# Routing of the second part of the expert stages: groups five blocks apart, loads one at a time, placing in two and sharing in five pieces

## What is computed

```python
h = _rms(x, ff_ln_w)
logits = h @ wg
...
gate = jax.nn.softmax(topv, -1)
...
weights = jnp.zeros_like(logits).at[bidx, sidx, topi].set(gate)
a = jax.nn.silu(jnp.einsum('bsd,edh->bseh', h, w1)) * jnp.einsum('bsd,edh->bseh', h, w3)
y = jnp.einsum('bseh,ehd->bsed', a, w2)
moe = jnp.einsum('bsed,bse->bsd', y, weights)
return x + moe
```

## Time and profile before

| What | Value |
|---|---|
| Median of three runs | 2684.96 us (2683.85 to 2685.91) |
| The profiled execution | 2682.36 us, its span 2680.6 us |
| Instructions | 60407 |
| TensorE busy | 2266.7 us, 85% |
| VectorE busy | 1855.2 us, 69% |
| ScalarE busy | 1159.6 us, 43% |
| GpSimd busy | 1103.8 us, 41% |
| Mean granted clock of TensorE | 0.90 |

### The profile page before, as it was taken

The page is one execution under the profiler, slowest core; times in us unless marked ns, Lnnn a source line. Parts: engine busy times, 40 slices in busy tenths (PEclk is TensorE's granted clock), DMA queues, the critical chain, the costliest instruction groups (busy, mean ns, idle before and its releaser), DMA issues. The chain is left out here.

```text
span 2680.6 us, 60407 instructions
## 1 busy us (share of the span) xinstructions
PE 2266.7 (85%) x20880; PEld 1718.4 (64%) x20880; DVE 1855.2 (69%) x3965; ACT 1159.6 (43%) x2509; POOL 1103.8 (41%) x1111
## 2 busy tenths in 40 slices
PE   6899999885887689995799998999988698999990
PEld 4555555543766567773577877777767577887770
DVE  4888888872556757765778788788787365445754
ACT  2676667664533223333344444444333263333330
POOL 3454445464153500000454454455477600224626
PEclk9897779865888889997999999999989799999995
DMA  5455555442368431201322323322334472446754
GB/s 118 120 115 129 143 129 135 114 125 87 113 215 252 150 134 41 60 29 40 88 66 75 84 66 78 81 72 73 76 96 116 136 240 79 138 137 184 234 159 144
DMA packets 249859, 313.10 MB, mean 117 GB/s; under 512 B 45152, under 2 KB 202848, under 8 KB 249056
## 3 DMA queue, kind: packets, MB, share of 16 engines
q1 hardware_dynamic: 188592, 219.11, 29.3%
q0 software_dynamic: 26624, 58.79, 8.0%
q10 hardware_dynamic: 34352, 31.34, 3.5%
HBM read 122.40 MB, written 102.24 MB: 84 GB/s over the span
## 5 line engine op out<-in xcount | busy, mean ns | idle before, releaser
L2084 POOL TENSOR_TENSOR ca_qk<-ca_qk,ca_q_swap 128x512 f32<-128x512 f32 x160 | 249.3, 1558 | 366.5 <-DVE ca_q_swap L2262 366.2
L731 DVE TENSOR_REDUCE soft_top<-soft_pa 128x2 fp32r<-128x512 f32 x512 | 328.1, 683 | 101.2 <-PE soft_pa L811 98.1
L626 ACT ACTIVATE soft_prob<-soft_pb 128x512 f32<-128x512 f32 x512 | 285.7, 594 | 190.4 <-PE soft_pb L804 187.9
L804 PE MATMUL soft_pb<-soft_rep 25*128 25x256 f32 x1024 | 210.2, 378 | 46.5 <-DVE soft_top L731 27.0
L804 PEld LDWEIGHTS soft_pb<-soft_rep 25*128 25x128 f32 x1024 | 137.3, 225 | 169.6 <-issue 85.3
L1416 PE MATMUL moe_pgu<-moe_w_hi,moe_xt_hi 128*128 x472 | 196.1, 415 | 38.9 <-DVE moe_xt_lo L1333 30.1
L811 PE MATMUL soft_pa<-soft_rep 24*128 24x256 f32 x1024 | 219.2, 384 | 5.8 <-DVE soft_top L731 3.5
L1435 PE MATMUL moe_py<-moe_w_d,moe_at 128*128 x788 | 217.8, 392 | 1.5 <-issue 0.8
L1338 DVE TENSOR_TENSOR moe_act_f<-moe_silu,moe_pgu 128x256 f32<-128x256 f32 (+1 forms) x236 | 88.4, 375 | 151.0 <-ACT moe_silu L1253 150.4
L2353 PE MATMUL ca_py<-ca_w_hi,ca_ot_hi 128*128 128x256 f32 x512 | 157.6, 308 | 35.0 <-DVE ca_ot_lo L2283 34.8
L1253 ACT ACTIVATE moe_silu<-moe_pgu 128x256 f32<-128x256 f32 (+1 forms) x236 | 82.1, 348 | 230.6 <-PE moe_pgu L1416 230.3
(11 more groups left out here) (377 smaller groups left out, 6376.3 us busy)
## 6 DMA issues: line engine op xcount, KB each, us to landing
ca_q_swap<-ca_q_f SPq DMA_DIRECT2D x640, 64.0 KB
moe_xs<-moe_rows SPq DMA_DIRECT2D x236, 128.0 KB, 2.1
soft_rep<-soft_parts SPq DMA_DIRECT2D x378, 64.0 KB
moe_rows<-soft_blank SPq DMA_DIRECT2D x27, 768.0 KB, 3.7
moe_ys_rows<-moe_ys ACTq DMA_DIRECT2D x134, 128.0 KB, 1.7
moe_ys<-moe_ys ACTq DMA_DIRECT2D x102, 128.0 KB, 2.3
moe_xd<-scratch SPq DMA_DIRECT2D x64, 128.0 KB, 2.6
ca_vs<-ca_v SPq DMA_DIRECT2D x32, 256.0 KB, 3.7
```

The source lines that it names most:

```text
L626: act.activation(prob[:, k % 4, h, :], p_b[:, 2 * T * h:2 * T * (h + 1)], ACT.Exp).then_inc(prob_ready, 1)
L731: dve.tensor_reduce(heads[:, j, :, g], p_a[:, 2 * T * h:2 * T * (h + 1)].rearrange("p (c s) -> p c s", c=HALF), AX, ALU.max).then_inc(a_do ...
L804: mm = pe.matmul(p_b[:, out], rep[of, i % 4, g, at:at + PART], rep[of, i % 4, g, 0:T], start=True, stop=True)
L2084: pool.tensor_tensor(qk[:, u % 2, m, :], qk[:, u % 2, m, :], q_swap[:, p % 2, :], ALU.add).then_inc(qk_ready, 1)
```

## The change

In both expert stages `place` is split in two: the half that gives each expert its first slot, and `place_rows`, which gives each row its slot and lets the sends begin. In `experts` the second half (with `limits`) runs one step after the first; in the attention stages the two halves run in the same step, as before. `weigh` is split into its pieces: `share` in step WEIGH, one `share_of` in each of the next TOP steps, `name_experts` in the step after. GpSimd's pace of sends starts one step after PLACE and ends where it did.

In `moe1` the groups come five steps apart (`PACE`), MEASURE starts at step 18, and each group's load is issued by SP five steps ahead of its MEASURE: in steps 13, 18 and 23, only the first behind the wait for `wlo_ready`. This puts MEASURE on 18, 23, 28; TURN on 20, 21, 25, 26, 30, 31; GRADE on 22, 27, 32; CHOOSE on 23, 28, 33; RANK on 35, PLACE on 36, the rows' slots on 37, the map on 38, sharing on 40 to 45. In `moe0` the groups stay three apart; RANK is now 14 in place of 15, so placing is on 15 and 16, the map on 17 and sharing on 19 to 22.

```diff
--- before.py
+++ after.py
@@ -280,6 +280,10 @@
         dve.wait_ge(route, ticks.n)
         dve.tensor_scalar(self.base[:], self.base[:], float(PART), 1.0, ALU.mult, ALU.add).then_inc(route, ticks.one())
         dve.tensor_reduce(self.passed[:], self.ended[:], AX, ALU.add).then_inc(self.passed_ready, 1)
+
+    def place_rows(self, dve):
+
+        E, n, route, ticks = self.EXPERTS, self.n, self.route, self.ticks
         dve.wait_ge(route, ticks.n)
         dve.tensor_tensor(self.key[:], self.kept[:, E:].rearrange("p (t e) -> p t e", e=E),
                           self.base[:].unsqueeze(1).to_broadcast([PART, n, E]), ALU.add).then_inc(route, ticks.one())
@@ -768,6 +772,7 @@
                         route.tally(dve)
                     if i == RANK + 1:
                         route.place(dve)
+                        route.place_rows(dve)
                     if i == RANK + 3:
                         route.weigh(dve)
                     t = i - 1
@@ -1038,9 +1043,10 @@
         stored = [sem(f"stored{i}") for i in range(SUMS)]
 
 
-        behind = lambda b, first: next((g for g in range(GROUPS) if b == first + 3 * g), None)
-        MEASURE, SCALE, TURN, GRADE, CHOOSE = ((-2 if AHEAD else EXPERTS - 1) + i for i in (0, 1, 2, 4, 5))
-        RANK = CHOOSE + 3 * GROUPS
+        PACE = 3 if AHEAD else 5
+        behind = lambda b, first: next((g for g in range(GROUPS) if b == first + PACE * g), None)
+        MEASURE, SCALE, TURN, GRADE, CHOOSE = ((-2 if AHEAD else EXPERTS + 2) + i for i in (0, 1, 2, 4, 5))
+        RANK = CHOOSE + PACE * (GROUPS - 1) + 2
         PLACE, MAP, WEIGH = RANK + 1, RANK + 3, RANK + 5
 
         if then is not None:
@@ -1125,10 +1131,10 @@
                         load_new(b + 3)
                     if b == (-1 if AHEAD else 2):
                         route.load(sp)
-                    if not AHEAD and b + 3 == EXPERTS:
-                        sp.wait_ge(wlo_ready, EXPERTS)
-                        for g in range(GROUPS):
-                            load_new(g)
+                    g = behind(b, MEASURE - 5)
+                    if not AHEAD and g is not None:
+                        past(sp, wlo_ready, 0 if g else EXPERTS)
+                        load_new(g)
                     if b == START[1]:
                         for t in range(SUMS):
                             load_sum(t)
@@ -1140,8 +1146,7 @@
                         store_sum(t)
                     if then is not None:
                         prepare(b - START[1])
-                behind = [t for t in (combined_behind(b) for b in range(ALL)) if t is not None]
-                for t in behind:
+                for t in [t for t in (combined_behind(b) for b in range(ALL)) if t is not None]:
                     if t not in [combined_behind(b - STORE_LAG) for b in range(ALL)]:
                         store_sum(t)
                     if t not in [combined_behind(b - LOAD_LAG) for b in range(ALL)] and t + SUMS < TILES:
@@ -1177,7 +1182,7 @@
                         bounds_check=SLOTS[h] - 1, oob_is_err=False
                     ).then_inc(yg_in[t % HELD], 16)
 
-                route.send(pool, 0, NEW * TOP, (y_ready, PLACE, START[1] - PLACE - 4))
+                route.send(pool, 0, NEW * TOP, (y_ready, PLACE + 1, START[1] - PLACE - 5))
                 pool.wait_ge(route.sent, 16 * NEW * TOP)
                 written(pool, START[1])
                 for t in tiles_of(0):
@@ -1298,9 +1303,15 @@
                             route.tally(dve)
                     if b == PLACE:
                         route.place(dve)
+                    if b == PLACE + 1:
+                        route.place_rows(dve)
                         route.limits(dve, until[:], START[1] + 3, until_ready)
                     if b == WEIGH:
-                        route.weigh(dve)
+                        route.share(dve)
+                    if b - WEIGH - 1 in range(TOP):
+                        route.share_of(dve, b - WEIGH - 1)
+                    if b == WEIGH + TOP + 1:
+                        route.name_experts(dve)
                         if norm == "layer":
                             dve.wait_ge(route.wk_ready, TOP)
                             dve.tensor_scalar(wk[:], wk[:], gate[:], None, ALU.mult).then_inc(gated, 1)
```

## The result

The changed kernel takes 2669.11 us (median of 12 runs, 2652.16 to 2678.82) where the kernel before, in 12 runs beside it, takes 2682.91 (2676.94 to 2698.95). The ratio is 0.994, 95% interval 0.9921 to 0.9960: 11 to 21 us less. The forecast of 10.4 us less is a ratio of 0.9961 and lies just outside; rival A, 13.8 us less, is 0.9949 and lies inside. Of the 2684.96 us from which the forecast counted, 0.994 is 2668.9, just under the low end of its range, 2669. The direction was right, the size too small.

What follows compares the result with a forecast made beforehand. TensorE was taken as the bound, its long waits in the second expert stage's routed stretch paid again in clock. Terms -3.0 - 5.2 + 7.5 - 3.4 - 6.3 = -10.4 us took 2684.96 to 2674.6 us, range 2669 to 2681.

Steps and rivals of the forecast that it cites:

- rival A: Second expert stage: the clock holds through both 1.8 us idles; 13.8 us less, 2671.2 us; chance 0.23.
- The clock after the meetings: Steps 23 and 28, measure and choice in one step: clock falls after each 1.8 us idle, costing 1.7 us each.
- 2 x 2.04 us: Steps 23 and 28: measure plus choice take VectorE 3.77 us, 1.73 free, so TensorE is delayed 2.04 us twice.
- nearest row: Earlier profile's 1.84 us idle, followed by clock 0.57; taken as nearest to the expected 1.8 us, hence a fall each.
- the reading of the Trainium skill: Recent activity lifts the clock, so a short hole need not lower it; by that alone the sum is 3.4 us better.
- Loads: Block 17's rows behind one load, not three: wait 4.25 to 0.9 us, gain 5.2 us; later loads cost nothing.
- Placing: Second stage, placing in two: wait 3.6 us shrinks, 1.6 us idle left, 0.3 us cost next step; gain 3.4 us.
- Sharing: Second stage, sharing in five pieces, all under 1.73 us and so free; 4.3 us wait gone, gain 6.3 us.
- First stage: First expert stage: GpSimd's sends start 1.0 us earlier and their two waits save 2.0 us; gain 3.0 us.
- The sum: Whole kernel: terms add to 10.4 us less, 2674.6 us for the median; chance 0.5.
- Groups: Second stage, groups five blocks apart: measure and choice meet in steps 23 and 28; cost 7.5 us.

Runs made afterwards that it cites:

- groups four apart: Changed kernel with the second stage's groups four blocks apart in place of five; ratio to the kernel before 0.9923 (0.9893 to 0.9954).
- splitting alone: Kernel before with placing and sharing split in both expert stages and RANK one step earlier, groups and loads as before; ratio to before 0.9917.
- loads alone: Kernel before with the three loads of new rows issued in SP's steps 13, 15 and 17 instead of all in 13; 2690.58 us, one run.
- loads behind the next rows: Changed kernel with each load of new rows one SP step later (14, 19, 24); 2667.81 us, one run.
- placing one block later: Changed kernel with the second stage's placing, map and sharing one step later after the ranking; 2672.17 us, one run.

## Why the prediction was right or wrong

**The clock after the meetings: the failed step.** "I take a fall each, 1.7 us" put 3.4 us into the sum that weren't there. The delay of 2 x 2.04 us came as worked out (waits of 1.83 and 1.80; without them, in the kernel with groups four apart, 4.0 us less). But a nearest row is one throw: the earlier trace rows show one fall after 1.84 us and none after 1.62, and were read as a boundary. In the second stage's stretch of all profiles a wait of 1.79 to 1.83 us was followed by a lower clock in 2 of 12 cases. That is rival A, and by these counts it should have had the larger chance. The sentence that weighed the reading of the Trainium skill (TensorE: Matmul & The Clock Gate, What's actually happening) against that row had the better answer, though that reading doesn't tell the 2 cases from the 10 either, and what does stays open.

**Loads.** 5.2 us were forecast; the interval of block 14 shrank by 4.2. The wait left is 1.32 and not 0.9 us, and the 0.4 us of issue behind it stayed. Nor was TensorE busy throughout the low clock after this wait, as the prediction has it, but for 3.03 of 3.40 us:

```profile
2192.00:2195.40 3.40, 3.03 (x9) 2.15 (x8) 0.42 (x1) 0.38 (x1) 0.00 (x0) 0.50 0.15 47
```

That the later loads cost nothing held.

**Placing.** The wait went from 3.6 to 1.54 us (forecast 1.6), the second half cost 0.3 in the next block, the clock held. As worked out, with its reason: the part that is due to ScalarE's late step went away when placing moved on by a block. In the kernel before, that step shows on ScalarE as a table load of 1.28 us, and on VectorE as a wait for ScalarE of as much ahead of placing:

```profile
2248.61 1.28 ACT L1253 ACT_TABLE_LOAD   x1
...
2250.32 0.42 DVE L1338 TENSOR_TENSOR moe_act_f<-moe_silu,moe_pgu 128x256 f32<-128x256 f32 x1 [1.27 <-ACT moe_silu L1253]
```

**Sharing.** All five pieces free. The two blocks that held the sharing took 7.31 and 4.29 us before, against 2.69 for a plain one: 6.2 us won, clock included (forecast 6.3). As worked out.

**First stage.** 3.1 us against 3.0, from the sends' start and their two waits; what TensorE won was given back, as the earlier trace rows let expect.

**The sum.** With no falls and the load at 4.2 the terms give -3.0 - 4.2 + 4.1 - 3.4 - 6.3 = -12.8 us; the two stretches measured give -13.0. The medians are 13.8 us apart and the ratio's middle is 16; its interval holds 13.0, and no run assigns the rest to anything. The low end of the range, 2669, took A and little else; the runs' own scatter, several microseconds from the unchanged stages, was counted with one.

**Groups.** That the pace of five is by itself a loss was in the forecast; what the forecast did not draw from it is that the same code with four would gain 4 us more.

## What to carry to other kernels

Count for each step of a hand-written order how long the helper engine may be busy before the bound engine feels it, by one row with its wait; then split long chains to fit under it, and check that two pieces never fall into one step when the pace changes. An engine's time won ahead of a wait for another engine's chain is given back there, so price such a half by that chain's start and its gaps. Put a bulk load behind the next small one that is due, not ahead of it.

## What the runs showed of the hardware

Whether the clock fell to its low level after a wait was not settled by the wait's length alone, though longer waits were followed by a fall more often. In the second expert stage's dense blocks, over the twelve profiles: waits of 1.1 to 1.5 us, 1 fall in 14; 1.79 to 1.83 us, 2 in 12; 2.58 and 3.23 us, both; 3.58 us and more, 8 in 9, the exception being one of 3.58. What tells the cases of one length apart, these runs don't show.

The low clock lasted 3.4 us in eleven of these thirteen falls, after waits of any of these lengths, and 6.8 us in two: after the 4.40 us wait in the kernel with splitting alone, and around the 4.33 us wait in the one with loads alone. What a fall of 3.4 us costs shows where traces differ in two blocks by it alone: the two behind the meeting in step 23 took 7.48 and 7.47 us with a fall after a wait of 1.81 us (loads behind the next rows, placing one block later), and 5.80 in the changed kernel without, so 1.7 us. A forecast can price a wait with the share of falls at its length, and a fall with 1.7 us or, as in two of thirteen, more.
